# Finishing the rotated queries and keys one step later, and the reciprocal of the softmax sums ahead of the first projection product

## What is computed

```
qkv = x @ Wqkv;  q, k, v = split(qkv)          # x: tokens shifted by half their channels
q = l2norm(q) * qs;  k = l2norm(k) * ksc
q = q * cos * scale + rotate_half(q) * sin * scale
k = k * cos * inv + rotate_half(k) * sin * inv
sim = einsum(q, k of two windows) * 8, masked
out = softmax(sim) @ v;  x = out @ Wo + x
x = (a * gelu(gate)) @ W2 + b2 + x             # a, gate from a layernorm of x
```

## Time and profile before

| | |
|---|---|
| median of 3 runs | 5493.87 us (5483.84 to 5496.69) |
| the profiled run | 5499.49 us, span 5497.7 us |
| PE busy over the span | 4684.0 us (85%) |
| DVE | 3694.6 us (67%) |
| ACT | 3155.3 us (57%) |
| POOL | 2034.8 us (37%) |
| transfers into `c_QK` | 3072, issued between 1868.5 and 5397.8 us |

### The profile page before, as it was taken

The page is one execution under the profiler, slowest core; times in us unless marked ns, Lnnn a source line. Parts: engine busy times, 40 slices in busy tenths (PEclk is TensorE's granted clock), DMA queues, the critical chain, the costliest instruction groups (busy, mean ns, idle before and its releaser), DMA issues. The chain is left out here.

```text
span 5497.7 us, 160430 instructions
## 1 busy us (share of the span) xinstructions
PE 4684.0 (85%) x63808; PEld 2744.8 (50%) x63808; DVE 3694.6 (67%) x5172; ACT 3155.3 (57%) x9549; POOL 2034.8 (37%) x1438
## 2 busy tenths in 40 slices
PE   7888888777777689989999899988998899999986
PEld 3333333322222356556666566655665566566553
DVE  5666677533333477777777777777777777777773
ACT  4444444323232367766776677666776766666774
POOL 2222222200000255554555455544555455545551
PEclk9999999877777799999999999999999999999997
DMA  1000000000000333344333433334333433343332
GB/s 45 0 0 0 0 0 0 24 0 0 0 0 0 98 87 87 84 97 94 86 86 91 97 85 87 85 92 96 86 88 93 98 84 87 90 97 86 85 85 74
DMA packets 197282, 340.10 MB, mean 62 GB/s; under 512 B 63568, under 2 KB 63568, under 8 KB 195024
## 3 DMA queue, kind: packets, MB, share of 16 engines
q1 hardware_dynamic: 196560, 330.14, 25.5%
HBM read 34.19 MB, written 6.29 MB: 7 GB/s over the span
## 5 line engine op out<-in xcount | busy, mean ns | idle before, releaser
L377 ACT ACTIVATE c_Pb<-c_S,c_nb 128x64 f32<-128x64 f32 x3072 | 918.0, 325 | 853.6 <-DVE c_nb L663 853.0
L342 POOL TENSOR_TENSOR c_F<-c_tAB 128x1024 f32<-128x1024 f32 x384 | 906.9, 2362 | 367.3 <-DMA c_QK<-c_F 213.8
L330 POOL TENSOR_TENSOR c_Pb<-c_Pb,c_rs 128x512 f32<-128x512 f32 x384 | 400.4, 1043 | 1426.0 <-DVE c_rs L671 1426.0
L644 DVE SCALAR_TENSOR_TENSOR c_tAB<-c_PA,c_WP,c_base 128x1024 f32<-128x1024 f32 x384 | 492.2, 1282 | 306.2 <-PE c_PA L450 305.9
L377 ACT ACTIVATION_READ_ACCUMULATOR c_Pb<-c_S,c_nb 128x1 f32 x3072 | 666.3, 217 | 0.0
L644 DVE SCALAR_TENSOR_TENSOR c_tAB<-c_PB,c_WP,c_base 128x1024 f32<-128x1024 f32 x384 | 491.6, 1280 | 58.8 <-PE c_PB L450 57.1
L334 POOL TENSOR_TENSOR c_sq<-c_sq 128x512 f32<-128x512 f32 x384 | 501.6, 1306 | 3.3 <-issue 2.4
L525 PE MATMUL c_S<-c_PTs,c_VE 64*64 64x32 f32 x10752 | 430.6, 222 | 62.3 <-DVE c_PTs L677 28.9
L659 DVE COPY c_VO<-c_PB 128x512 f32<-128x512 f32 x384 | 263.9, 687 | 320.4 <-PE c_PB L485 320.1
L651 DVE SCALAR_TENSOR_TENSOR c_F<-c_PD,c_F 128x1024 f32<-128x1024 f32 x384 | 466.6, 1215 | 9.0 <-ACT c_PD L368 8.8
L525 PE MATMUL c_S<-c_PTs,c_VO 64*64 64x32 f32 x13824 | 442.9, 222 | 22.8 <-issue 22.1
(11 more groups left out here) (247 smaller groups left out, 9597.9 us busy)
## 6 DMA issues: line engine op xcount, KB each, us to landing
c_QK<-c_F SPq DMA_DIRECT2D x3072, 64.0 KB, 2.0
c_VE<-c_VO SPq DMA_DIRECT2D x384, 128.0 KB
c_VE<-c_VO SPq DMA_DIRECT2D x384, 96.0 KB
c_stage<-in_w_heads SPq DMA_DIRECT2D x24, 256.0 KB, 2.9
c_WT<-in_w_tails SPq DMA_DIRECT2D x6, 1024.0 KB, 6.7
a_W<-in_w_level SPq DMA_DIRECT2D x1, 3335.5 KB, 10.7
c_WT<-in_w_tails SPq DMA_DIRECT2D x6, 537.5 KB, 4.3
b_W<-in_w_level SPq DMA_DIRECT2D x1, 3133.0 KB, 10.2
```

What stands on the lines that cost most here:

```text
L330: nc.gpsimd.tensor_tensor(p, p, rs[:, n % 2, :].unsqueeze(2).broadcast_to([P, HS, KEYS]), ALU.mult).then_inc(*p_ready.up())
L342: nc.gpsimd.tensor_tensor(F[:, j % 2], tAB[:, j % 2, 0], tAB[:, j % 2, 1], ALU.add).then_inc(*rotated.up())
L377: e = nc.scalar.activation(Pb[:, n % 2, i, :], S[:, n % 2, r, c * KEYS:(c + 1) * KEYS], ACT.Exp, bias=nb[:, n % 2, r * PS + c:r * PS + c + ...
L644: nc.vector.scalar_tensor_tensor(out=tAB[:, kind, half], in0=bank[:, :].unsqueeze(1).broadcast_to([P, 2, SEQ]), scalar=WP[:, 2 * kind + ha ...
```

## The change

On DVE the finishing product moves from step n, where it stood for job n-3 just ahead of `pt_copy`, to the next step, where it stands right behind `row_max` (job n-4). On SP the transfers of that job move along, and stand ahead of the shift of values. On DVE `inv_sum` moves ahead of the first of the two `products`.

```
+        def job_finished(n, now, nxt):
+            return (n - 4) % NS, nxt if n >= 4 else now
+
...
                 def step(n, now, nxt, prev, new, fresh):
-                    jb, tb = job_before(n, now, nxt)
+                    jf, tf = job_finished(n, now, nxt)
                     v, tv = v_unit(n, now, nxt)
+                    if tf:
+                        permute(jf, tf)
                     if v % 2 and tv:
                         shift_values(v // 4, v % 4 // 2, tv)
-                    if tb:
-                        permute(jb, tb)
...
                     j, tj = job(n, now, nxt)
-                    jb, tb = job_before(n, now, nxt)
+                    jf, tf = job_finished(n, now, nxt)
                     v, tv = v_unit(n, now, nxt)
...
                     if now:
                         row_max(n, now)
+                    if tf:
+                        finish(jf, tf)
                     if prev and n == 2:
                         residual(prev)
...
                     if tv:
                         v_copy(v, tv)
+                    if now:
+                        inv_sum(n, now)
                     if tj:
                         products(j, 0, tj)
-                    if now:
-                        inv_sum(n, now)
...
                     if tj:
                         products(j, 1, tj)
-                    if tb:
-                        finish(jb, tb)
                     if now:
                         pt_copy(n, now)
```

## The result

| | before | after |
|---|---|---|
| median | 5490.15 us (5483.84 to 5496.69, 4 runs) | 5772.88 us (5766.0 to 5791.31, 4 runs) |
| ratio, 95% interval | | 1.052 (1.0492 to 1.0548) |
| profiled run | 5499.49 us | 5771.66 us |

The change makes the kernel 5.2% slower, 282.7 us or 5.9 us for each of the 48 turns.

A forecast was written before the change was run, and what follows sets the result against it. PE bounds the kernel, busy 66.07 of 72.02 us a turn. 47 turns at 5.85 us each are 275, plus 4 for the last turn; 5499 + 279 = 5778 us, range 5640 to 5875.

The forecast's parts named there:

- The length of the path: From the row maximum, through finishing product, eight transfers, `rotate` and `add_squares`, to the next step's `sumsq`: at least 12.64 us.
- Step 2: `sumsq` on PE waits for the late `rotate` and `add_squares`; PE stands 2.75 us, so step 3 starts 2.55 later.
- Steps 0 and 1 cost nothing: Finishing product of step 0 falls into DVE's idle time, `sumsq` of step 1 hardly waits; bounded by 0 and 0.5 us.
- Step 3: Job 7 finishes late, the scores of step 4 wait for its transfers about 3 us; step 4 is 4.2 us late.
- no longer, only later: SP's queue: the eight transfers keep their place relative to the four of `shift_values`, so the queue gets only later.
- Step 4: Finishing product ahead of `scale` and the values' copy delays PE's second projection 1.2 us, partly absorbed: +0.8, together 5.0.
- Step 5: `sumsq` can't start before 46.64, by the same path sum as before: +0.4, together 5.4.
- Step 7: `hidden` moves by 1.2 us and PE's product that waits for it starts later: +0.45, together 5.85.
- Step 6: Waits for ACT, whose gelu block follows the second projection of step 5; keeps the 5.4 and adds nothing.
- Hidden by ACT: In step 6 the reciprocal, moved ahead, holds up the products by 1.2 us, hidden by ACT; its cost taken as 0.
- The clock: Rival, chance 0.19: PE's new stands of 2.75 and 3 us drop the clock to half, adding 80 us: 5858 us.
- The two rivals: Slower only by the scores of step 4, 5640 us, chance 0.17; slower with a falling clock, 5858 us, chance 0.19.

The follow-up runs named there:

- three buffers: The changed kernel with a third buffer for `c_F` instead of two: 5763.81 us, ratio 1.049; the kernel before with the same third buffer: 5491.72 us, ratio 0.9991.
- jobs 3 and 7 at the old place: Finishing product one step on except for jobs 3 and 7, three buffers, reciprocal in its old place, SP sending behind the shift: 5655.8 us, ratio 1.029 to the kernel before.
- the product alone: The changed kernel with the reciprocal back behind the first product, two buffers: 5705.2 us, ratio 1.0378 to the kernel before.

## Why the prediction came out right, and where its steps did not

The forecast was 5778 us, and 5772.88 was measured; the profiled run became 272 us slower where the sum gave 279. The sum is right in total and not in its terms. Over the 25 turns of the table a turn became 5.3 us longer, forecast 5.85: steps 0 to 3 were put 2.4 us too high, steps 4 and 5 together 0.2 and step 6 1.7 too low. That these errors nearly cancel is luck.

**The length of the path was right.** 12.64 us were worked out from the row maximum of step 1 to the sum of squares of step 2; 13.36 are read in the turn above, 12.71 in the mean. `rotate` waits 23.6 us in the turn where "some 15" was forecast.

**Step 2, forecast +2.55, measured +0.54** (25.88 for 25.34). The step that failed is "Steps 0 and 1 cost nothing": the row maximum of step 1 comes at 8.93, not at 10.71. The row maximum stands behind the split of the next input, and with POOL idle in step 0, waiting for the transfers, when DVE comes to the split, this takes 0.42 + 0.69 us in place of 1.09 + 1.64 (medians of the 48 in each trace). The path starts 1.8 us earlier, and takes most of the stall away.

**Step 3, forecast to +4.2, measured +1.81** (35.91 for 34.10), both because step 3 begins earlier and because the scores start 6.50 us after the product in the turn read, where 7.3 was taken (6.99 in the mean). But this term, and not that of step 2, is the one that carries the loss. The three buffers take the stall of step 2 away and the time stays; with three buffers and the reciprocal in its old place, jobs 3 and 7 back at theirs, and sent first, take the wait of step 4 away, and the time is that of before. The prediction added the two; the runs show that what the first wait loses comes back at the second. It also had SP's queue as "no longer, only later". With three buffers that queue, and not the product, sets the scores of step 4, and in the run with jobs 3 and 7 at the old place it was worth 159 us.

**Step 4, forecast +0.8: measured -0.17.** The copy of the probabilities no longer stands behind the finishing product and starts 6.54 us after the row maximum in place of 7.09, a gain that the prediction set to 0. With the product alone it starts at 7.38, so the reciprocal has a part in this gain.

**Step 5, forecast +0.4: +1.6**, a mean step of 10.16 us in place of 8.57. The sum of squares starts 5.57 us after the row maximum in place of 3.88. Three buffers shorten this step to 7.69 us, so the buffer has a part; but with the product alone, on two buffers, the step takes 8.30 us, and step 4 in front of it 8.46. From the row maximum of step 4 to the sum of squares of step 5 there are 13.13 us in the changed kernel and 12.40 with the product alone, where the path was forecast at 12.64: what step 4 gains, step 5 loses again. Taken together the two steps are 1.4 us longer, forecast 1.2. **Step 7, forecast +0.45: +0.40**, right.

**Step 6, forecast 0: +1.7**, of which 0.7 is there with the product alone (11.49 us for 10.78); the exponentials end 0.4 us later there, and why was not followed. "Hidden by ACT" is the wrong step. ACT hides the first product's delay from the scaling on POOL, but not from what stands behind it on DVE, up to the copy of the probabilities. The reciprocal, forecast at 0, costs 95 us alone and 68 on top of the other edit.

**The clock** was a rival with 0.19, at 80 us, and the forecast said that PE's busy time would not change if the clock held. It did not hold, and PE's busy time rose by 104 us. The rival named the stands of steps 2 and 4, and the clock falls at the second; step 6, where more of the lower clock lies, it did not name. Its price shows in part: 101 us behind the scores of step 4 in the kernel with three buffers, 23 us in step 6 of the changed one. The page named in the prediction, the Trainium skill's TensorE: Matmul & The Clock Gate, section "HAM oscillation — how this bites in real kernels", agrees with the windows of step 4: the clock drops at the pause for transfers. The two rivals and the forecast were not alternatives; the late path, the scores' wait, its clock and the reciprocal all have a share in one sum. Of the mean 5.3 us a turn, the two edits alone have 3.6 and 2.1.

What stays open: how the 101 us divide in the changed kernel itself, whose wait in step 4 is shorter than with three buffers. And whether jobs 3 and 7 at the old place would be enough with two buffers was not run.

## What to carry to other kernels

Before a producer is moved, list the consumers that wait for its transfers, and count the issue of everything that its transfer queue has in front: four issues of 0.6 us decided over 159 us here. A wait that one more buffer takes away may only uncover the next wait for transfers on the same queue; follow the chain to the consumer that can't be moved before adding terms. A small row that waits for another engine belongs behind all rows of its engine that are ready earlier; ahead of them it cost nothing here only in those steps in which its input comes first.

## What the runs showed of the hardware

DVE's rows with their operands in SBUF depend on what POOL does beside them. In the changed kernel with three buffers, where POOL works in step 0, DVE and POOL read:

```profile
3968.47 1.24 DVE L636 CAST c_xh<-xf 128x512 fp32r<-128x512 f32 x1
3969.74 1.64 DVE L638 TENSOR_TENSOR c_xl<-xf,c_xh 128x512 fp32r<-128x512 f32 x1
```

```profile
3967.06 2.36 POOL L348 TENSOR_TENSOR c_F<-c_tAB 128x1024 f32<-128x1024 f32 x1 [1.89 <-DVE c_tAB L650]
3969.37 1.46 POOL L339 TENSOR_TENSOR c_sq<-c_sq 128x512 f32<-128x512 f32 x1
```

The cast takes 1.24 us beside `rotate`, and 0.42 in the changed kernel, where POOL is idle; the difference takes 1.64 and 0.69. The second row of `scale` has a median of 1.25 us before and 0.49 after. The finishing product, which reads one operand from PSUM, takes 1.21 in both, beside a POOL row or not.

What counts is which row starts first. In the changed kernel's turn the difference starts at 4140.38, and this `rotate` begins while it runs:

```profile
4140.51 2.78 POOL L345 TENSOR_TENSOR c_F<-c_tAB 128x1024 f32<-128x1024 f32 x1 [3.88 <-DMA c_QK<-c_F]
```

The difference keeps its 0.69 us, and `rotate` takes 2.78 where it took 2.37 before. In the 48 turns of the changed kernel the difference takes 0.69 us in the 44 in which no POOL row runs at its start, and 1.64 in the other 4. The kernel before has 47 turns of the second kind, also at 1.64. So a wait on POOL made rows on DVE shorter, and step 0 with them.

The Trainium skill, GPSIMD Engine Reference, section "Specifications", states that GpSimd shares its SBUF interfaces with VectorE, and contends with instructions that have two SBUF inputs or run in a two-port mode; the rows of the difference agree.

The granted clock fell behind the stretch in which PE was busy for 1.39 of 3.40 us, and stayed at 1.00 behind the one with 2.26, filled with useless products. Such products made the kernel with three buffers 101 us faster; in step 6 of the kernel before they won nothing.
